# Moving one PSUM-to-SBUF copy per sort step from ScalarE to VectorE in a graph-network kernel

## Time and profile before

| | us |
|---|---|
| median of 3 runs | 4822.65 (4818.04 to 4827.08) |
| profiled execution, its own time | 4810.64 |
| its span, first to last instruction | 4808.9 |
| busy PE / DVE / ACT / POOL | 3834.3 / 3239.0 / 1714.3 / 2386.6 |
| mean granted TensorE clock, of full speed | 0.90 |

### The profile page before, as it was taken

How to read it: one execution, slowest core, us unless ns; L and a number is a source line. 1 busy time by engine, 2 the same in 40 slices (tenths; PEclk the granted TensorE clock), 3 DMA queues, 4 the chain that set the end, 5 groups by cost and what they waited for, 6 DMA issues and landing times.

```text
span 4808.9 us, 111129 instructions
## 1 busy us (share of the span) xinstructions
PE 3834.3 (80%) x27568; PEld 2952.3 (61%) x27569; DVE 3239.0 (67%) x8054; ACT 1714.3 (36%) x4185; POOL 2386.6 (50%) x2369
## 2 busy tenths in 40 slices
PE   3589888889966666666678888998888998888997
PEld 2556655566645445555546667775667776666776
DVE  8858777777877777777745555665555765555666
ACT  0025555555511111111132224773222774222575
POOL 2877777777047777777700004770001773000675
PEclk9559898989987887788869999999999999999999
DMA  1111111111033232333317886774887773888676
GB/s 43 37 46 54 49 48 50 49 48 38 1 85 77 76 78 76 78 78 77 71 11 202 229 229 202 208 209 123 230 232 214 207 209 115 232 229 230 192 209 179
DMA packets 791567, 607.25 MB, mean 126 GB/s; under 512 B 172939, under 2 KB 703933, under 8 KB 791510
## 3 DMA queue, kind: packets, MB, share of 16 engines
q1 hardware_dynamic: 679798, 329.11, 24.7%
q0 software_dynamic: 111712, 277.47, 20.4%
HBM read 361.22 MB, written 245.08 MB: 126 GB/s over the span
## 4 chain that ended last, share of the span: by engine, by line
PE 41%; POOL 23%; issue 17%; DMA 7%; DVE 7%; SPq 1%; DVEq 1%; ACT 1%; POOLq 0%; ACTq 0%
PE ps L825 21%; PE ps L822 18%; POOL slot_rows L631 11%; POOL y_sb L642 10%; DMA mid<-msgs,block_idx 3%; POOL mid L654 3%; DMA iota_h<-codes 2%; DVE mid L1606 1%; DMA a_code<-codes 1%; DMA y_sb<-in_x_dram,idx_st 1%; DVE mid L1542 1%; SPq L571 1%; DVE y_sb L1274 1%; DVE mid L1622 0%; PE ps L913 0%
## 5 line engine op out<-in xcount | busy, mean ns | idle before, releaser
L654 POOL DMA_INDIRECT mid<-msgs,block_idx x750 | 715.4, 954 | 1654.2 <-DMA msgs<-mid 1408.0
L822 PE MATMUL ps<-mid 128*128 128x128 f32 (+3 forms) x7668 | 1234.2, 299 | 89.3 <-DMA mid<-msgs,block_idx 34.9
L666 ACT ACTIVATE mid<-ps 13x512 f16<-13x512 f16 (+3 forms) x1665 | 638.6, 399 | 1369.2 <-PE ps L825 900.7
L825 PE MATMUL ps<-y_sb,mid 128*128 x6552 | 943.5, 287 | 221.7 <-issue 137.3
L822 PEld LDWEIGHTS ps<-mid 128*128 128x128 f32 (+3 forms) x7668 | 857.7, 175 | 317.8 <-issue 263.4
L825 PEld LDWEIGHTS ps<-y_sb,mid 128*128 128x128 f32 x6552 | 792.7, 191 | 374.4 <-issue 374.2
L642 POOL DMA_INDIRECT y_sb<-in_x_dram,idx_st x808 | 790.7, 979 | 417.9 <-issue 250.3
L631 POOL DMA_INDIRECT slot_rows<-y_sb,row_st x784 | 862.9, 1101 | 265.6 <-issue 237.2
L1622 DVE TENSOR_SCALAR mid<-iota,slot_lo,slot_w 128x128 f32<-128x128 f32 x2250 | 664.1, 378 | 314.2 <-PE ps L822 302.4
L825 PE MATMUL ps<-y_sb 128*128 128x193 f32 x1616 | 434.3, 423 | 270.7 <-DVE mid L1542 186.5
L825 PEld LDWEIGHTS ps<-mid 100*128 100x128 f32 (+2 forms) x1884 | 349.9, 207 | 385.0 <-ACT mid L666 211.6
(11 more groups left out here) (246 smaller groups left out, 3357.6 us busy)
## 6 DMA issues: line engine op xcount, KB each, us to landing
msgs<-mid SPq DMA_DIRECT2D x819, 256.0 KB, 3.6
y_sb<-slot_rows SPq DMA_DIRECT2D x101, 268.0 KB, 3.2
a_code<-codes SPq DMA_DIRECT2D x411, 64.0 KB, 3.6
iota_h<-codes SPq DMA_DIRECT2D x408, 64.0 KB, 3.6
y_sb<-in_edge_attr_dram SPq DMA_DIRECT2D x54, 256.0 KB
y_sb<-in_x_dram,idx_st POOLq DMA_INDIRECT x808, 2.5
slot_rows<-y_sb,row_st POOLq DMA_INDIRECT x784
mid<-msgs,block_idx POOLq DMA_INDIRECT x750, 3.7
```

Of the source, the lines that this page charges most:

```text
L654: nc.gpsimd.indirect_dma_start(out=rows[:, s % RB, :], out_offset=None, in_=msg_blocks, in_offset=bass.IndirectOffsetOnAxis(ap=block_idx[: ...
L666: return nc.scalar.activation(o, i, func, **kw)
L822: return nc.tensor.matmul(o, a, b, start=False, stop=False, skip_group_check=True)
L825: return nc.tensor.matmul(o, a, b, start=True, stop=True, skip_group_check=True)
```

## The change

ACT no longer makes `same`; DVE does, with one `tensor_scalar` (add -12, then max with 0) from PSUM bank 6. It stands in DVE's order behind `take_looked` and `place`, ahead of `pick_lo`, `pick_ranked` and `pick_dst`, and waits for `paired` of the step ahead. Semaphores and PE's program stay the same, as does the GpSimd memset of `not_same`, which is now unused.

```diff
 @block.scalar
-            def copy_same(n, q):
-                act.wait_ge(S["paired"], n + 1)
-                copy(same[:, q, :], ps[:, 6, :], ACT.Relu, bias=not_same[:, 0:1]).then_inc(S["same_made"], 1)
-
...
                     copy_table(4 * n + 3, 1)
-                    if ahead:
-                        copy_same(n + 1, (b + 1) % 2)
 
             copy_bits(0, 0)
             copy_q(0, 0)
-            copy_same(0, 0)
...
 @block.vector
+            def take_same(n, q):
+
+                dve.wait_ge(S["paired"], n + 1)
+                v.tensor_scalar(same[:, q, :], ps[:, 6, :], float(1 - KEYBITS), 0.0, ALU.add, ALU.max
+                                ).then_inc(S["same_made"], 1)
+
...
                     if b == 0 and 1 <= g0 <= GROUPS:
                         place(g - 1, 1 - par)
+                    if g0 < GROUPS - 1 or (g0 < GROUPS and b < GB - 1):
+                        take_same(GB * g + (b + 1), (b + 1) % 2)
                     if b == 1 and 1 <= g0 <= GROUPS:
...
             for half in range(2):
                 pick_dst(0, 0, half)
+            take_same(0, 0)
             over_groups(sort_picks, dve, 2, ((2, GROUPS - 1),), GROUPS + 2)
```

## The result

The changed kernel takes 4827.05 us, median of 12 runs, against 4818.42 us for the kernel before in 12 runs beside it: ratio 1.0022, 95% interval [1.0014, 1.0031]. I had forecast no change, 3 us to the fast side; it is some 9 to 11 us slower (8.6 by the medians, 10.6 by the ratio). The 4820 us of the forecast were counted from 4822.65, a median of 3 runs; 12 runs put the kernel before 4 us lower. The profiled execution took 4833.06 us, with a span of 4831.3 against 4808.9 before.

What follows compares the result with a forecast made beforehand. Scatters were taken to bound about 38 groups of the sort, its own pace the last ten. Terms -1.7 - 5 + 4 gave about -3 us, so a median of 4820 us, within 0.2%; range 4806 to 4845.

Steps and rivals of the forecast that it cites:

- What bounds the kernel: In the sort: scatters on POOL set the pace for about 38 groups, then PE, ACT and DVE for ten.
- What leaves ACT: ACT's queue: removing the 0.68 us copy starts builds earlier, covering two late POOL starts; 1.7 us gained, bounds 0 and 1.7.
- What DVE gains in work: DVE's queue: 0.60 us per copy plus a wait make PE fall behind in the last groups; about 4 us lost.
- The clock rival: Tail of the sort: PE gaps at group starts lower the granted clock, about 18 us slower, 4838; chance 0.10.
- What the scatters gain: Scatters in 38 groups: later picks come in longer runs and delay scatters 0.14 us less per group; 5 us gained.
- The port rival: POOL: the copy's PSUM read stops scatters as picks do, 26 us slower, 4846, mean scatter 1.12 us; chance 0.12.
- a new timing of the picks that simply meets scatters oftener: POOL's scatters: slower because retimed DVE picks meet them more often; no size of its own, chance 0.04.

Runs made afterwards that it cites:

- act_short: Kernel before the change with ScalarE's copy cut to 32 of 512 columns, the others staying zero; ratio 1.0007.
- wait_only: Kernel before the change with DVE also waiting for the pairs where the change puts the copy, ScalarE still copying; ratio 1.0100.
- after_again: The changed kernel run again on another chip, against the kernel before; ratio 1.0028.
- wait_psum2: wait_only with one needless read of 510 PSUM values on DVE ahead of `take_looked` in step 2 of each group; ratio 1.0009 to the kernel before.
- same_after_lo: Changed kernel with copy and wait moved behind `pick_lo`, ahead of `pick_ranked`, in step 1 only; ratio 1.0043 to the kernel before.
- split_after: Changed kernel with each 128x2048 one-hot made by two instructions of 128x1024; ratio 1.0036 to the kernel before.
- same_mid: Changed kernel with the copy of step n in DVE's own step n, between picks and `take_looked`; ratio 0.9972 to the kernel before, 0.9992 on another chip.
- split_onehots: Kernel before the change with each 128x2048 one-hot made by two instructions of 128x1024; ratio 0.9974.

## Why the prediction was wrong

**What bounds the kernel** held: the scatter until group 39 (38 before), then PE and DVE. The chain's last wait was to stay in group 38; it moved to 39.

**What leaves ACT** held, and its size nearly: the scatter that started at 366.10 starts at 364.85, so 1.25 us were gained of the 1.7; act_short, 1.0007 with 1 inside its interval, shows no gain of that size. What the prediction says of ScalarE as the cheaper reader of PSUM isn't seen: the copy takes 0.68 us on either engine (196 times each).

**What DVE gains in work** held in kind. The copy takes 679 ns and stands 0.60 us in a row (1050.38 to 1050.98). DVE is busy 17.46 of 17.60 us. The last groups take 17.47 to 17.56 us, 0.12 to 0.18 more than before where I had 0.25, the four ahead of them 2.0 us more together where I had 2.2, and the tail 2.8 us more where I had 4. PE waits for line 1237 at the starts, though the profile names that line at few of them. The clock rival did not come: 1.00 in all tail groups.

**What the scatters gain** is the step that failed, in size and in sign. I put the loss per scatter down to the picks, and let scatters meet them at a random phase: 0.106 us for a pick alone, 0.073 for one followed by another, nine pieces becoming five, so 5 us gained. The runs show four things in its place:

- *The row behind the step was misread.* The scatter of 1.49 us at 540.17 ends at 541.66. I put that down to the pick that starts 0.56 us into it. But DVE had been in a 128x2048 one-hot since 539.60:

```profile
539.60 1.22 DVE L1244 TENSOR_TENSOR y_sb<-y_sb,mid 128x2048 f16<-128x2048 f16 x1
```

It ends at 540.82, and 0.84 later the scatter ends. The pick began when the scatter was already held.

- *The loss lay elsewhere.* Of 67.1 us lost before, 12.4 were beside picks and 44.5 beside the 128x2048 one-hots of line 1244, which the step did not consider. That my sum came near, 1.47 against 1.7 per group, was chance. The timeline of before had a scatter of 1.56 us, 0.49 us into the one-hot, at 29 of the one-hots of step 2.
- *The phase isn't random.* A held scatter goes on at the end of a DVE instruction, ends 0.84 later, and the next starts 0.30 after that: the two engines fall into step. In a run of picks 0.50 us apart the next scatter starts 1.14 = 2 x 0.50 + 0.14 behind a pick's end, is held to the end of the pick that is running, and so on: each takes 1.20, 0.23 lost. Runs of four without gaps, which I had counted as the better case, are the worse. Before, 276 of 636 picks stood alone and lost 0.012 us each; after, the 144 runs of four lost 0.055 per pick, and the picks' loss grew from 12.4 to 33.1 us.
- *The wait shifts the one-hots.* wait_only lost 48 us by that alone, and added work that moved one of three one-hots by 0.2 us, or by 0.6 us through a read of PSUM, gave most of it back; six copies within SBUF did not (1.0136). The copy, which reads PSUM, acts in the same way: it puts step 2's one-hot behind the scatter's start (19.8 us lost before, 3.2 after), and so takes back most of what its own wait costs. In steps 1 and 3 the loss is 10.3 and 10.2 us above that of before.

Measured: 21 us more for the scatters in the profiled run, 13 in after_again's, where I had 5 less. Of that, what comes ahead of the last wait counts for the end of the sort.

**The port rival** gave the mean scatter I would have taken as its proof, 1.12 us (1127 and 1118 ns measured), for a cause that isn't there: the scatters beside PSUM reads lost 0.0 us in all after the change, and 0.4 at most in any run. The 0.04 that I had set aside for "a new timing of the picks that simply meets scatters oftener" was nearest to what happened.

**What stays open.** The rule tells what most scatters cost at a given phase, and for one step at a time it told the next phase (wait_psum2). Which phases a whole new order will lock into I could not tell beforehand (same_after_lo, split_after), and one kernel can lock differently on two chips (same_mid). Nor is it known when a scatter is let in between two DVE instructions and when it is held past both.

## What to carry to other kernels

Where GpSimd issues a long row of indirect DMAs and sets the pace, look at what VectorE does 0.1 us after each starts: two-input SBUF operations and picks held them to their end here, reads of PSUM didn't. Before a wait is put into VectorE's queue, ask what stands behind it: it turns loose instructions into runs, and runs fall into step with the scatters. Put work that waits for another engine where its wait is already over (same_mid), and judge such an edit by the scatters' total, with a second chip for anything below half a per cent.

## What I had not expected of the hardware

- An indirect DMA's issue of 0.97 us has a point about 0.1 us behind its start: with a 1.21-us one-hot beginning just after its start it takes 0.97, begun 0.1 us into one it takes 1.94.
- Between two DVE instructions without a gap it is mostly let in (64 of 65 between 128x1024 halves in split_onehots, and between picks, 1.20), but not always: 36 of 83 were held past both halves in split_after (1.77 us and more), others 2.48 us across six small copies and a one-hot, and up to 3.3 across a one-hot, a copy and two more.
- The lock holds for hundreds of microseconds: 38 of 41 one-hots of one step met a scatter at the same 0.1 us.
